# Local transformer block: the output projection moved into the middle of the scores' matmuls

## The reference, cut to what matters

```python
x = attn(shift_tokens(x)) + x
x = ffn(shift_tokens(x)) + x
# attn: 16 heads of 64, windows of 32 tokens, each looks at itself and the window before
q, k, v = split(x @ Wqkv)
q = rotary(l2norm(q) * q_scale);  k = rotary(l2norm(k) * k_scale)
sim = einsum('bhwie,bhwje->bhwij', q_window, k_two_windows) * 8   # masked
out = softmax(sim) @ v_two_windows
out = out @ Wo
# ffn: layernorm, then (xn @ W1a + b1a) * gelu(xn @ W1g + b1g) @ W2 + b2
```

## Time and profile before

| | us |
|---|---|
| three runs | 4346.51, 4351.18, 4365.92 |
| median | 4351.18 |
| the profiled execution | 4365.65 |
| its span, first to last instruction | 4363.4 |
| TensorE matmuls busy | 4042.2 (93%) |
| VectorE busy | 3355.2 (77%) |
| GpSimd busy | 2940.3 (67%) |
| ScalarE busy | 2584.6 (59%) |
| mean granted share of TensorE's clock | 0.966 |

### The profile page before, as it was taken

One profiled execution on the slowest core, in us unless ns is written; L12 is line 12 of the kernel. 1 busy time (PEld: TensorE's weight loads), 2 busy tenths in 40 slices (PEclk: granted clock), 3 DMA queues, 4 the chain that ended last, 5 costly groups with the idle time before them and its releaser, 6 DMA issues. The chain is left out here.

```text
span 4363.4 us, 151568 instructions
## 1 busy us (share of the span) xinstructions
PE 4042.2 (93%) x66856; PEld 2968.0 (68%) x66856; DVE 3355.2 (77%) x3997; ACT 2584.6 (59%) x3022; POOL 2940.3 (67%) x3465
## 2 busy tenths in 40 slices
PE   8989969999999999999968888699999999999997
PEld 5655557777777777777623333577877877787775
DVE  5635568887888888888658884788888888797885
ACT  4424436666666666667527775367666667666664
POOL 2202158888888888888524441688888888888884
PEclk9999989999999999999969998899999999999999
DMA  4304322332233232232100000323232233333221
GB/s 149 123 10 142 104 88 79 79 87 74 78 83 94 74 86 75 80 85 74 40 11 1 1 1 1 98 77 91 79 83 74 79 88 84 83 87 84 69 68 40
DMA packets 164542, 316.94 MB, mean 73 GB/s; under 512 B 38760, under 2 KB 42480, under 8 KB 156848
## 3 DMA queue, kind: packets, MB, share of 16 engines
q1 hardware_dynamic: 153520, 241.18, 20.6%
q0 software_dynamic: 10368, 66.06, 4.7%
HBM read 92.03 MB, written 20.05 MB: 26 GB/s over the span
## 5 line engine op out<-in xcount | busy, mean ns | idle before, releaser
L678 PE MATMUL psum<-loc_w_hl,loc_z_lo 128*128 128x512 f32 x1152 | 511.8, 444 | 34.8 <-DMA loc_w_hl<-parted 26.4
L924 ACT ACTIVATE loc_sq<-psum 128x1024 f32<-128x1024 f32 x192 | 196.6, 1024 | 470.5 <-PE psum L680 465.4
L1061 POOL TENSOR_TENSOR loc_rc_k<-loc_rc_k,loc_rs_k 128x1024 f32<-128x1024 f32 x192 | 454.3, 2366 | 21.4 <-DVE loc_rs_k L1189 21.4
L1175 DVE TENSOR_REDUCE loc_ssq<-loc_sq 128x16 f32<-128x1024 f32 x384 | 463.8, 1208 | 3.7 <-POOL loc_rn L1057 3.6
L1079 POOL TENSOR_TENSOR loc_prob<-loc_prob,loc_recip 128x1024 f32<-128x1024 f32 x192 | 365.6, 1904 | 140.8 <-DVE loc_recip L1212 140.0
L679 PE MATMUL psum<-loc_w_hl,loc_z_hi 128*128 128x512 f32 x1152 | 457.8, 397 | 2.7 <-issue 2.6
L1061 POOL TENSOR_TENSOR loc_rc_q<-loc_rc_q,loc_rs_q 128x1024 f32<-128x1024 f32 x192 | 460.0, 2396 | 0.0
L680 PE MATMUL psum<-loc_w_hl,loc_z_hi 128*128 128x512 f32 x1152 | 458.2, 398 | 1.9 <-issue 1.9
L775 PE MATMUL psum<-loc_PT,loc_V 64*64 64x32 f32 x24576 | 405.6, 220 | 14.3 <-issue 13.4
L775 PEld LDWEIGHTS psum<-loc_PT,loc_V 64*64 64x64 f32 x24576 | 381.5, 135 | 40.0 <-issue 16.6
L795 PEld LDWEIGHTS psum<-loc_outT,loc_wo 128*128 128x128 f32 x3072 | 376.3, 193 | 19.3 <-issue 2.7
(11 more groups left out here) (199 smaller groups left out, 9728.5 us busy)
## 6 DMA issues: line engine op xcount, KB each, us to landing
loc_V<-loc_V SPq DMA_DIRECT2D x1152, 128.0 KB
loc_V<-loc_V SPq DMA_DIRECT2D x672, 64.0 KB
loc_w_hl<-parted POOLq DMA_DIRECT2D x36, 1024.0 KB, 7.7
parted<-moe_halves POOLq DMA_DIRECT2D x18, 1024.0 KB, 5.2
moe_spread<-moe_gates SPq DMA_DIRECT2D x64, 256.0 KB, 4.1
moe_raw<-in_wqkv POOLq DMA_DIRECT2D x18, 512.0 KB, 5.9
moe_w<-in_moe_w SPq DMA_DIRECT2D x32, 256.0 KB, 3.3
loc_wo<-in_wo SPq DMA_DIRECT2D x12, 512.0 KB, 3.6
```

The costliest lines, as they stand in the source:

```text
L678: pe.matmul(M.bank[bank + g], z_lo[:, r, tokens], w_hl[:, k, 0, cols], start=True, stop=False)
L1061: pool.tensor_tensor(rc, rc, rs[:, :], ALU.add).then_inc(added, 1)
L1175: dve.tensor_reduce(ssq[:, a:a + HEADS], heads(sq[:, :]), AX_X, ALU.add).then_inc(totalled, 1)
```

## The change

`scores` is cut into `mask_scores` and a `scores` that takes a range of head pairs. In a step TensorE now does the mask matmuls, the first 64 small matmuls, the output projection of tile n-3, and the other 64 small matmuls; only these raise `s_full`. The output projection's old place, between `project_k` and `values`, is empty. It belonged to tile n-4 and the new one to tile n-3 of the step before, so each tile's projection comes half a group of scores and a `project_k` earlier than it did. Other engines' lists are as they were.

```diff
-            def scores(L, t):
+            def mask_scores(L, t):
                 i = t % TILES
                 pe.wait_ge(qT_ready, upto(L, t))
...
                 pe.wait_ge(kT_ready, upto(L, t))
                 pe.sem_inc(pe_passed, 1)
-                for p in range(PAIRS):
+
+            def scores(L, t, first, end):
+                i = t % TILES
+                for p in range(first, end):
                     for w in range(TILES):
                         for c in range(2):
...
-                mm.then_inc(s_full, 1)
+                if end == PAIRS:
+                    mm.then_inc(s_full, 1)
...
                 if live(n):
                     project_k(L, n, live(n - 3))
-                if live(n - 4):
-                    output(L, n - 4)
                 if live(n - 3):
                     values(L, n - 3, live(n - 1))
...
                 if live(n - 2):
                     turn_probs(L, n - 2, live(n - 1))
                 if live(n - 1):
-                    scores(L, n - 1)
+                    mask_scores(L, n - 1)
+                    scores(L, n - 1, 0, PAIRS // 2)
+                if live(n - 3):
+                    output(L, n - 3)
+                if live(n - 1):
+                    scores(L, n - 1, PAIRS // 2, PAIRS)
```

## The result

| | us |
|---|---|
| the changed kernel, median of 4 runs | 4519.81 (4517.4 to 4525.4) |
| the kernel before, beside it | 4355.48 (4346.51 to 4365.92) |
| ratio, 95% interval | 1.0371 [1.0346, 1.0396] |
| span of the profiled execution | 4519.5 (before 4363.4) |
| mean granted share of TensorE's clock | 0.968 (before 0.966) |

The change makes the kernel 3.7% slower. The forecast was +3.4%, 4500 us. Times and ratios, here and in the experiments, are of fast executions, which leaves out one of experiment 12 (8444 us, granted clock 0.661).

The account below looks back on a forecast made before the run. TensorE, 93% busy, bounds the kernel while others answer in time. List and waits 1.34 - 0.46 - 0.12 + 0.08 = +0.84 us a step, +150 us: 4500 us, +3.4%; own range +0.45 to +1.15, 4435 to 4565; 8 in 10, 4385 to 4570.

Parts of the forecast that it names:

- The old place gives back 1.78 us: TensorE, from the scores' end to `values`: 1.78 us quicker once the output projection leaves, 1.88 less 0.10 for small tiles.
- The scores grow by 2.08: TensorE, first small matmul to scores' end: 3.58 us, 2.08 more, with the projection inside; its list grows 0.30 a step.
- `project_q` waits for `copy_out` until S + 6.12: n mod 4 = 0 and 3: ScalarE's copy holds TensorE 1.11 us, S being the scores' end; step +1.41 us.
- `turn_q` waits for `copy_v`: n mod 4 = 2: ScalarE's Gelu load, GELU and copy hold TensorE about 0.93 us; step +1.23 us.
- `turn_probs` waits for `normalise`: n mod 4 = 1: VectorE's chain, then `normalise`, hold TensorE 1.0 us, bound 1.7; step +1.3 us.
- The holes come back: TensorE's instruction-supply idle time: 0.46 us a step regained in scores, 0.12 in `values` hidden by waits, 0.08 charged for new holes.
- `add_attention` gets its input earlier: VectorE's `add_attention`: the projection's result comes earlier after the change; no cost was charged.
- The output's own waits, bound 0.1: Output projection in its new place, waiting for bank 7's users on VectorE: no cost, bound 0.1.
- A drain behind the table load: Rival, ScalarE: table switches cost 1.4 us more without a gap before `copy_out`; about +1 a step, some 4700 us; chance 0.02.
- TensorE's list alone: Rival: the waits are covered and TensorE's list decides, -0.08 to -0.36 us a step, 4280 to 4335 us; chance 0.09.
- Waits and savings that nearly cancel: Rival: half of the waits are real, at most +0.27 us a step, 4340 to 4400 us; chance 0.1.
- More than that: Rival: VectorE's or GpSimd's chain also holds `turn_probs` in every kind of step, another 0.4 a step, 4575 us or more; chance 0.07.

Follow-up runs that it names:

- experiment 12: Changed kernel with the output projection behind two of the eight head pairs instead of four: 4518.23 us, ratio 1.0356.
- experiment 1: Changed kernel with ScalarE's local GELU replaced by Identity, so no Gelu table loads: 4440.01 us, ratio 1.0193.
- experiment 3: Changed kernel with the FFN pieces `variance` and `lin` 1 moved ahead of `project_v` and `project_q`: 4864.72 us, ratio 1.1166.
- experiment 4: Changed kernel with VectorE's `add_attention` one step earlier, just ahead of `maximum`: 4470.88 us, ratio 1.0243.
- experiment 5: Changed kernel with `add_attention` one step earlier and GELU replaced by Identity: 4370.05 us, ratio 1.0015.
- experiment 6: Changed kernel, real GELU, `add_attention` early, `cut_tokens` behind `invert`, GELU 2 later, `copy_v` ahead of GELU 1, `lin` 1 ahead of `project_v`: 4403.58 us, ratio 1.0079.
- experiment 7: The kernel of experiment 6 with VectorE's `add_ffn` also moved ahead of `floored`: 4385.87 us, ratio 1.0062.
- experiment 9: Kernel before with `cut_tokens` behind `invert` and GELU 2 at the end of step n mod 4 = 2: 4354.42 us, ratio 0.9978.

## Why the prediction was right, step by step

A clean step is taken here as the tenth percentile of its kind, a mean step with all its holes. Both are worked out from the same 160 full steps of the two traces as S to S. Times behind S are medians of their kind of step.

| n mod 4 | clean before | clean after | rise | predicted |
|---|---|---|---|---|
| 0 | 16.26 | 17.78 | +1.52 | +1.41 |
| 1 | 15.20 | 16.49 | +1.29 | +1.3 |
| 2 | 15.38 | 16.64 | +1.26 | +1.23 |
| 3 | 15.37 | 16.82 | +1.45 | +1.41 |
| mean, clean | 15.55 | 16.93 | +1.38 | +1.34 |
| mean, with holes | 16.29 | 17.12 | +0.83 | +0.84 |

- *The old place gives back 1.78 us.* `values` started at S + 3.30 and starts at S + 1.52. Exact.
- *The scores grow by 2.08.* They take 3.63 us from first to last, +2.14 on 1.49. So TensorE's list grew by 0.36 us a step, 69 us, not 0.30. The Trainium skill, in "TensorEngine Tiling (Array Packing)", section Tiling Modes, says that a mode switch drains the engine. This agrees in kind; but the prediction's estimate of 20 us, from the drain in "TensorE: Matmul & The Clock Gate", Part 2, is under a third of the 69.
- *`project_q` waits for `copy_out` until S + 6.12.* It starts at S + 5.99, where without the wait it would start at S + 5.01: 0.98 us of waiting, not 1.11. *`turn_q` waits for `copy_v`* until S + 9.00 in n mod 4 = 2 (predicted 9.03). *`turn_probs` waits for `normalise`* until S + 11.43 in n mod 4 = 1 (predicted 10.28 + 1.0 = 11.28), and in the median of no other kind. All three are in the waits above.
- *The clean rises agree within 0.11 us a step, in part because errors cancel.* In n mod 4 = 3 the list is 0.06 longer than predicted and the wait 0.13 shorter, and 0.13 us that the prediction did not have come behind the wait: from `project_q` to `turn_q` it is 3.22 us where it was 3.09. n mod 4 = 0 has the same 0.12 between `project_q` and `variance` (1.49 for 1.37).
- *The holes come back.* 1.38 - 0.83 = 0.55 us a step against 0.50 predicted. In the local blocks TensorE's idle time without a releaser sums to 82.5 us before and 28.5 after: 54 us, 0.28 a step. The 26 us of it that now stand in `values` (0.14 a step) fall ahead of the new waits, which can hide them, as the prediction had it; how much they do hide, and the rest of the 0.55, is not worked out from a run. The fear that the holes only move to the values was half right: 14.3 to 28.4 us.
- *"`add_attention` gets its input earlier"*, no cost: this step was incomplete. The input came earlier and `add_attention` did not. It stands behind the k chain on VectorE and ends about 7.3 us after S (3144.92 in the step shown), and `variance` needs it. `variance` starts at S + 7.48 after the change; in experiment 1, where the wait for `copy_out` is gone and `add_attention` alone decides, it starts at S + 7.46. Two chains that end 0.02 us apart cost no more than one: the forecast was spared this one by luck. Experiments 1 and 3 uncovered it, 4 and 5 priced it. The 0.06 us that experiment 4 gives in n mod 4 = 0 are about half of the largest error of the table.
- *The output's own waits, bound 0.1:* 0.0 us after the change; it is a third chain right behind the others (experiments 5 to 7).
- The size: 0.83 us on 192 steps is 159 us where 150 stood, because the forecast counted 186 steps and took off for the layers' starts. The two blocks grew by 162 us (first scores to last, 3074.9 to 3236.9), the whole by 164.
- The stated range's top, +1.15 us a step, is not what its two terms give (0.84 + 0.25 + 0.15 = 1.24); the +0.83 measured is well inside either.

The rivals fell one by one. A drain behind the table load isn't seen: 0.01 us. TensorE's list alone would have given 4280 to 4335; experiment 7 takes the waits away and still has 4386. That is where the estimate of the list and the holes fails: +0.36 us of list a step, 69 us, and holes of 45.5 us in place of 82.5, -37, make +32 us; 25 are measured (35 in the two blocks of the trace). Without the waits the split does not even pay for itself. So of the 164 us of the change about 139 are waits (127 by the lengths of the two blocks), and 134 were taken away by moving six pieces of work, five of them on other engines. Two of the six give the kernel before 10 us as well (experiment 9), `copy_v`'s costs it about 1%, and three were not tried there, so not all of the 134 need be the change's own. Waits and savings that nearly cancel is what happens only after those repairs. "More than that" needed `turn_probs` to wait in every kind of step, and it does so, in the median, in one.

## What to carry to other kernels

When TensorE reaches a wait sooner, ask when the signal it waits for can come at all: price the move from the last common event (here the end of the scores) along each other engine's chain, and the step grows by the latest of them, not by the change of TensorE's own list. Behind the wait that you find, look for the next one: here two chains ended 0.02 us apart in n mod 4 = 0, and taking away either alone gave 0.00 or 0.06 us in that kind of step. Moving work ahead to fill a wait is no remedy as long as that work has a wait of its own: in experiment 3 it cost 345 us. Work that splits a long run of small matmuls does take holes out of it, but it has a price of its own: here 69 us of list against 37 of holes once the waits are gone. And a move by one place on another engine, such as `copy_v`'s in the kernel before, can cost 1% by what stands behind it.

## What the runs showed of the hardware beside this

- TensorE's holes without a releaser have a strict place. Count its matmuls, weight loads and sequencer instructions in order: in the local blocks of all fourteen traces every such hole over 0.3 us stands at the same count modulo 256, and work resumes 1.0 to 1.6 us (median 1.4) after the end of a 16 KB packet of the instruction queue. An output projection between the halves cut them from 60.9 to 0.2 us at the scores; once the waits were gone too (experiment 7) 14.8 us were back there.
- A small VectorE operation on 32 columns took from 0.17 to 2.05 us, depending on what GpSimd did beside it. After the change 94 of the 192 start while a large two-input operation of GpSimd is under way. They take 1.86 us on average, and every one ends within 0.1 us of GpSimd's; the other 98 take 0.55. In the kernel before, 111 start so, but later in GpSimd's operation, and take 1.15. So the mean went from 819 ns before to this after, 72 us more on VectorE for 192 instructions, without a change to either list, because the two had shifted against each other:

```profile
L1187 DVE TENSOR_SCALAR loc_ssq<-loc_ssq 128x32 f32<-128x32 f32 x192 | 229.4, 1195 | 11.2 <-DVE loc_ssq L1182 0.5
```
